# Position products of the two convolutional attentions: queries also kept with image row and column exchanged, every copy made by GpSimd

## The reference, cut to what matters

```
r_q = q.reshape(b, NH, h, w, hd)
rel_h = jnp.einsum('bnhwc,hkc->bnhwk', r_q, Rh)
rel_w = jnp.einsum('bnhwc,wkc->bnhwk', r_q, Rw)
bias = (rel_h[..., :, None] + rel_w[..., None, :]).reshape(b, NH, hw, hw)
attn = jnp.einsum('bnqd,bnkd->bnqk', q, k) * scale + bias
```

## Time and profile before

| | |
|---|---|
| Median of three runs | 3370.66 us |
| The profiled execution's own time | 3370.78 us |
| Its span | 3368.9 us |
| Busy | TensorE matmul 2764.8, VectorE 2414.6, ScalarE 1860.7, GpSimd 435.2 us |
| Mean granted TensorE clock | 0.882 |
| c0: first position product, last one, first load of the next stage | 97.3, 183.1, 195.63 us |
| c1: the same | 1288.2, 1374.3, 1386.79 us |

### The profile page before, as it was taken

How to read it: one execution, slowest core, us unless ns; L and a number is a source line. 1 busy time by engine, 2 the same in 40 slices (tenths; PEclk the granted TensorE clock), 3 DMA queues, 4 the chain that set the end, 5 groups by cost and what they waited for, 6 DMA issues and landing times. The chain is left out here.

```text
span 3368.9 us, 62705 instructions
## 1 busy us (share of the span) xinstructions
PE 2764.8 (82%) x18708; PEld 1277.7 (38%) x18708; DVE 2414.6 (72%) x4597; ACT 1860.7 (55%) x2592; POOL 435.2 (13%) x513
## 2 busy tenths in 40 slices
PE   5948999997499239589999956199999959599999
PEld 3612222226499126222222234022222236366666
DVE  6458999974766354579999955589999835465665
ACT  4416777773255124167777736067777736465554
POOL 0010111111333510101111110201111100000000
PEclk9759999996699667599999977599999979699999
DMA  2555776664122214567766701101111110200000
GB/s 64 169 125 114 151 148 142 148 126 143 33 78 76 70 31 146 134 110 150 149 146 149 145 22 50 57 28 52 48 48 49 48 32 1 55 22 5 9 5 14
DMA packets 202070, 277.27 MB, mean 82 GB/s; under 512 B 54302, under 2 KB 93454, under 8 KB 201930
## 3 DMA queue, kind: packets, MB, share of 16 engines
q1 hardware_dynamic: 162346, 211.32, 27.1%
q0 software_dynamic: 19920, 31.57, 4.0%
q10 hardware_dynamic: 19664, 32.60, 3.3%
HBM read 196.93 MB, written 77.46 MB: 81 GB/s over the span
## 5 line engine op out<-in xcount | busy, mean ns | idle before, releaser
L750 DVE TENSOR_REDUCE c1att_mx<-c1att_m 128x1 f32<-128x512 f32 x768 | 493.4, 685 | 35.7 <-PE c1att_m L688 30.6
L750 DVE TENSOR_REDUCE c0att_mx<-c0att_m 128x1 f32<-128x512 f32 x768 | 493.4, 685 | 32.5 <-PE c0att_m L688 27.2
L750 DVE TENSOR_REDUCE f1att_mx<-f1att_m 128x1 f32<-128x512 f32 x768 | 493.3, 685 | 26.5 <-PE f1att_m L688 21.8
L996 ACT ACTIVATE c1att_p<-c1att_s 128x1024 f32<-128x1024 f32 x384 | 373.9, 1020 | 152.0 <-PE c1att_s L703 151.9
L996 ACT ACTIVATE c0att_p<-c0att_s 128x1024 f32<-128x1024 f32 x384 | 373.9, 1020 | 148.8 <-PE c0att_s L703 148.7
L996 ACT ACTIVATE f1att_p<-f1att_s 128x1024 f32<-128x1024 f32 x384 | 373.9, 1020 | 143.8 <-PE f1att_s L703 142.8
L1426 ACT ACTIVATE moe_h<-moe_u,moe_bu 128x512 f32<-128x512 f32 x192 | 136.5, 711 | 175.6 <-PE moe_u L1343 93.9
L688 PE MATMUL f1att_m<-f1att_km,f1att_qm 16*128 16x512 f16 x768 | 155.7, 401 | 88.6 <-DVE f1att_ka L959 52.9
L716 PE MATMUL f1att_o<-f1att_p,f1att_vs 128*32 128x512 f32 x1536 | 206.2, 609 | 0.6 <-ACT f1att_p L996 0.6
L716 PE MATMUL c0att_o<-c0att_p,c0att_vs 128*32 128x512 f32 x1536 | 206.2, 609 | 0.6 <-ACT c0att_p L996 0.6
L716 PE MATMUL c1att_o<-c1att_p,c1att_vs 128*32 128x512 f32 x1536 | 206.1, 609 | 0.6 <-ACT c1att_p L996 0.6
(11 more groups left out here) (608 smaller groups left out, 5430.8 us busy)
## 6 DMA issues: line engine op xcount, KB each, us to landing
xt<-rel_parts SPq DMA_DIRECT2D x256, 128.0 KB, 5.0
xt<-qk_parts SPq DMA_DIRECT2D x192, 128.0 KB, 4.4
y<-rel_parts SPq DMA_DIRECT2D x128, 128.0 KB, 5.6
y<-qk_parts SPq DMA_DIRECT2D x96, 128.0 KB, 5.1
c0att_qm<-rel_parts SPq DMA_DIRECT2D x144, 64.0 KB, 2.1
c1att_qm<-rel_parts SPq DMA_DIRECT2D x144, 64.0 KB, 2.1
expert_rows<-y SPq DMA_DIRECT2D x39, 192.0 KB, 2.0
o_sums<-c0att_o ACTq DMA_DIRECT2D x24, 256.0 KB, 4.3
```

What stands on the lines that cost most here:

```text
L750: dve.tensor_reduce(mx[:, n:n + 1], bank[:, :], AX.X, ALU.max).then_inc(s_mx, 1)
L996: act.activation(pr[h][kt % 2][:, :], sps[h][:, :], ACT.Exp).then_inc(s_e, 1)
```

## The change

The stage keeps a second set of the queries, `by_x`, in which each quarter is stored column by column. It lies in `parts`, whose chunk c is free once the chunk's matmuls are done. Rows 0 to 63 of `by_x[g]` take the high part, rows 64 to 127 the low part (which comes from rows 0 to 63 of `low`). GpSimd makes all 48 copies of 64 x 512 elements. The table `th[1]` holds its values in both halves of its rows, by one more ScalarE activation, so one matmul gives high table by (high + low) query. For k = 1 two matmuls take the place of three, and they read runs of 16 neighbouring elements. TensorE waits, at the beginning of each (g, 1), for the copies of that group's last chunk.

```
+        s_byx = [m.sem(f"byx{k}") for k in range(2)]
+        by_x = parts
+        def by_columns(t, c):
+            return t[:, c * CHUNK:(c + 1) * CHUNK].rearrange("p (s x y) -> p s x y", s=2, x=QSIDE)
+        def by_rows(t, c, g):
+            return t[0:GW, at(c, g)].rearrange("p (s y x) -> p s x y", s=2, y=QSIDE)
@@ GpSimd
-                for i, t in enumerate(th + tl if rel else ()):
+                if not rel:
+                    return
+                for i, t in enumerate((th[0], tl[0], tl[1])):
                     pool.memset(t[GW:P, :], 0.0).then_inc(s_zero, 1)
                     pool.wait_ge(s_zero, i + 2)
+                for c in range(CHUNKS):
+                    pool.wait_ge(s_v, 4 * c + 4)
+                    for g in range(GROUPS):
+                        pool.wait_ge(s_hi, c * GROUPS + g + 1)
+                        pool.tensor_copy(by_columns(by_x[g][0:GW, :], c), by_rows(high, c, g)).then_inc(s_byx[0], 1)
+                        pool.wait_ge(s_lo, c * GROUPS + g + 1)
+                        pool.tensor_copy(by_columns(by_x[g][GW:P, :], c), by_rows(low, c, g)).then_inc(s_byx[1], 1)
@@ TensorE
-                pe.wait_ge(s_zero, 5)
+                pe.wait_ge(s_zero, 4)
+                pe.wait_ge(s_wh, 5)
...
                     for k in range(2):
+                        if k:
+                            for part in s_byx:
+                                pe.wait_ge(part, (CHUNKS - 1) * GROUPS + g + 1)
...
-                                pe.matmul(out, wh, row_of(top, k, r), start=True, stop=False)
-                                pe.matmul(out, wl, row_of(top, k, r), start=False, stop=False)
-                                ins = pe.matmul(out, wh, row_of(rest, k, r), start=False, stop=True)
+                                if k:
+                                    both = column_of(by_x[g], r)
+                                    pe.matmul(out, wh, both, start=True, stop=False)
+                                    ins = pe.matmul(out, wl, both, start=False, stop=True)
+                                    continue
+                                pe.matmul(out, wh, row_of(top, r), start=True, stop=False)
+                                pe.matmul(out, wl, row_of(top, r), start=False, stop=False)
+                                ins = pe.matmul(out, wh, row_of(rest, r), start=False, stop=True)
@@ ScalarE
+                        act.activation(th[1][GW:P, :], tab[1][:, :], ACT.Identity).then_inc(s_wh, 1)
@@
+def column_of(q, r):
+    return q.rearrange("p (n s x y) -> p s x n y", s=2, x=QSIDE, y=QSIDE)[:, r // QSIDE, r % QSIDE]
```

More of the change, by code:

```diff
@@ L492, in _, with row_of @@
                     store_rel(act, GROUPS - 1, 1, qq // 2, qq % 2, 0, rhi)
[L495 to L499, removed]
+def row_of(q, r):
+    return q.rearrange("p (b u s y x) -> p u y b s x", b=B, u=2, s=2, y=QSIDE)[:, r // QSIDE, r % QSIDE]
+def column_of(q, r):
+    return q.rearrange("p (n s x y) -> p s x n y", s=2, x=QSIDE, y=QSIDE)[:, r // QSIDE, r % QSIDE]
 def row_bank(bank, k, j):
```

## The result

The changed kernel takes 3337.62 us (median of 4 runs, 3336.11 to 3344.65), the one before 3371.62 us (4 runs) beside it: ratio 0.9902, 95% interval 0.9886 to 0.9918. The forecast was 3332 us with a range of 3316 to 3360. The span fell from 3368.9 to 3334.5 us, by 34.4.

The account below looks back on a forecast made before the run. TensorE's k = 1 matmuls, reading elements 32 bytes apart, were taken to bound the position products. Saving 19.6 us in each of c0 and c1, 39.2 in all, took 3370.8 to 3332 us, range 3316 to 3360.

Parts of the forecast that it names:

- The copy: GpSimd's 48 copies a stage: 1.10 us each, 0.92 for stepped reads at 1.80 ns an element plus 0.18 fixed.
- the lower bound: GpSimd's copy without any penalty for the 32-byte step: 512 x 0.83 ns + 180 ns = 0.61 us.
- B: Rival: GpSimd copies of 1.5 us; gain only 6.5 us a stage, 3358 us; chance 0.15.
- C: Rival: GpSimd copies of 1.97 us; slower, 3399 us; break-even where the 44th copy ends at 149 us; chance 0.11.
- D: Rival: the step costs GpSimd nothing, copies of 0.61 us; gain 27 us a stage, 3317 us; chance 0.13.
- The lock: Chunk phase: GpSimd copies and VectorE's two-SBUF-input `low` exclude each other for whole instructions, 1.10 + 0.69 = 1.79 us a unit.
- rival A: GpSimd takes two turns to VectorE's one in the chunk phase; gain 11.2 us a stage, 3348 us; chance 0.14.
- The chunk phase: VectorE's 24 units cost 0.16 us more each, 3.8 us in all; the phase ends at 101 us instead of 97.
- All 96 stores lie behind 126 us: End of the stage: 48 stores from each queue take 44.8 us at 281 GB/s, ending at 171.3 us.
- The wait at g = 2: ScalarE's wait for the stores of (0, 0) is over by then, as SP issues them from 126 to 134 us.
- Runs of 16: TensorE's k = 1 matmuls: 0.06 to 0.11 us instead of 0.23, so 67 us of a stage shrink to about 16.
- Rival E: k = 1 matmuls get only fewer, not faster; gain 4.3 us a stage, 3362 us; chance 0.05 with other no-change ways.

Follow-up runs that it names:

- e1: Changed kernel with copies in row order, so k = 1 matmuls read with the 32-byte step again: 3344.61 us, ratio 0.9909 to the kernel before.
- e9: Changed kernel with GpSimd's copies begun only after all 24 remainders (`low`) of the chunk phase: 3380.49 us, ratio 1.0013 to the kernel before.
- e3: Changed kernel with VectorE making the 24 low-part copies, GpSimd only the high-part ones: 3349.13 us, ratio 0.9917 to the kernel before.
- e2: Changed kernel with a third k = 1 matmul, by a table of zeros, back in each row: 3338.88 us, ratio 0.9887 to the kernel before.
- e5: Changed kernel with the query and key scratch laid out so a store's target is one run of 64 rows: 3293.14 us, ratio 0.9767.
- e6: Kernel before the change with only the query and key store layout of one 64-row run: 3344.13 us, ratio 0.9921 to the kernel before.
- e4: Changed kernel in the order (0,0), (1,0), (0,1), (1,1), (2,0), (2,1): 3335.52 us, ratio 0.9887 to the kernel before.
- the first four experiments: e1, e2, e3 and e9, each an edit of the changed kernel, run on one chip: ratios 0.9909, 0.9887, 0.9917 and 1.0013.

## Why the prediction was right, and where it was off

| step, c0 | predicted | measured |
|---|---|---|
| a copy alone | 1.10 us | 1.09 to 1.11 |
| copy and `low` together | 1.79 us | 1.52 |
| first product | 101 us | 102.1 |
| (0, 1) begins | 125 | 121.08 |
| SP's 48 remainder stores | 44.3 us | 44.4 |
| next stage | 176 | 176.60 |
| gain in c0, c1 | 19.6, 19.6 us | 19.0, 12.3 |

**The copy.** The choice between 0.61 and 1.97 us, on which four of the six cases hung, was right. e1 shows the lower bound to be the exact price without the step, 0.61, so the step costs about 0.48 us in 512 elements: (1.09 - 0.18) / 512 = 1.78 ns each against 0.84. By the 2.9 cycles an element of the Trainium skill, GPSIMD Engine Reference, section Performance pitfalls for Q7 kernels, it would have been 1.42 us, an estimate; the measurement decides against that for a plain copy. Its surcharge of one cycle for the step agrees (0.94 ns, 1.1 of the 1.2 GHz cycles of that estimate). Rivals B, C and D fall with it. e9 moved the start of (0, 1) late by another way, and the change broke even about where C said.

The time of c0 is a weaker test of this price than it looks. SP's remainders go out behind its first 48 stores, and these end at 128.4 us with the change, at 131.4, 128.8 and 128.3 in e1, e3 and e9, however long the copies take. In e3 (0, 1) begins at 125.7 instead of 121.1 us and the stage takes 119.8 us instead of 118.2. So any price that brings the 44th copy in before about 126 us should have given nearly this time; it is the copies' own durations that bear the price out.

**The lock.** The collision is there, as e9 shows, and it spares the values (L450), which take 0.34 us as before. A copy and a `low` on their own make 1.10 + 0.69 = 1.79 us, the pair takes 1.52: the two instructions overlap for 0.27 us and do not exclude each other for their whole length. That is against my reading of the earlier trace rows. The Trainium skill, SBUF — State Buffer, section Who interferes with whom, calls it an exclusive lock; taken for the whole of both instructions, the trace does not bear that out. Of the 0.27 us up to 0.18 could be the copy's fixed part, so whether the two still take turns while they move elements stays open. Nor did GpSimd take two turns to one (rival A): copies and `low` alternate one to one. The 44th copy was done at 121.0 us, 4 us sooner than forecast.

**The chunk phase.** 3.8 us were forecast for an even slowing, and the last `low` came 4.1 us later. The sum was right, its parts not. Three pairs make 4.56 us, which is less than the 4.89 us that a chunk took before, so the steady phase isn't slower. The delay arises in the first chunks: 2.2 us at chunk 1's first `low`, 3.7 at chunk 2's, 5.0 at chunk 3's, of which 1.0 comes back. The first part can be read on VectorE's timeline and ScalarE's:

```profile
61.61 1.09 DVE L459 TENSOR_TENSOR c0qkv_low<-c0qkv_qt,c0qkv_high 128x512 f16<-128x512 f32 x1 [0.54 <-ACT c0qkv_high L496]
...
62.90 2.29 DVE L466 TENSOR_TENSOR c0qkv_tab<-c0qkv_raw,c0qkv_own 64x252 f32<-64x252 f32 x2
...
67.88 1.15 DVE L459 TENSOR_TENSOR c0qkv_low<-c0qkv_qt,c0qkv_high 128x512 f16<-128x512 f32 x1 [2.42 <-ACT c0qkv_high L496]
...
72.25 1.39 DVE L472 TENSOR_TENSOR c0qkv_tl<-c0qkv_tab,c0qkv_th 64x252 f16<-64x252 f32 x2
```

```profile
65.22 0.72 ACT L501 ACTIVATE c0qkv_th<-c0qkv_tab 64x252 f16<-64x252 f32 x2 [3.64 <-DVE c0qkv_tab L466]
65.96 0.41 ACT L502 ACTIVATE c0qkv_th<-c0qkv_tab 64x252 f16<-64x252 f32 x1
```

The same instructions of VectorE in the kernel before:

```profile
62.79 0.73 DVE L438 TENSOR_TENSOR c0qkv_tab<-c0qkv_raw,c0qkv_own 64x252 f32<-64x252 f32 x2
...
69.18 0.73 DVE L444 TENSOR_TENSOR c0qkv_tl<-c0qkv_tab,c0qkv_th 64x252 f16<-64x252 f32 x2
```

VectorE's two products for the tables (L466, L438 before) also have two inputs in SBUF. They took 0.73 us before and take 2.29 beside the first copies. ScalarE waits 3.64 us for them where it waited 1.68, and the new activation adds 0.41. I had written that the copies collide with the `low` and with nothing else in this stage; this was the other thing, and I had left it at nothing. Of chunk 2's further 1.5 us the tables' remainders (L472, L444 before) make 0.66. Chunk 3's further 1.3 us come from the pairs: chunk 2 had taken 3.52 us from `low` to `low` before, less than three pairs, and takes 4.81 now. These are readings of the two timelines; no run takes one of them away.

**The end.** "All 96 stores lie behind 126 us" was the step that gave the result, and it holds but for ScalarE's first four. ScalarE's share began at 122 and SP's at 128.4, and SP's 48 took the forecast time, at 1.09, 0.89 and 0.79 us each rather than at an even 0.92. e2 shows that a third matmul doesn't count in it, e5 that the stores do, and e6 that they did not before the change. The wait at g = 2 was not over, as I had said; ScalarE stood for 1.87 us:

```profile
145.63 0.60 ACT L516 ACTIVATE c0qkv_rhi<-c0qkv_rp 128x512 f16<-128x512 f32 x1 [1.87 <-DMA rel_parts<-c0qkv_rlo]
```

It lies beside transfers at a share of 0.92, while SP's queue runs on without a gap, so it can have cost little.

**Runs of 16.** The premise that they make the k = 1 matmuls cheap is right: 0.055 us at the high clock and 0.11 at the low one, against 0.23. The inference that the gain comes from it was not tested in the prediction, and e1 refutes it for this kernel: with the step left in and one matmul of three gone the time is the same. Rival E had priced that at 4.3 us a stage, since it let (0, 1) begin at 125 us; copies without the step let it begin at 103.4. The exchange makes matmuls cheap and copies dear in equal measure at this bound.

**The missing 4.8 us.** The forecast named a gain of 39.2 us, the spans show 34.4. c0 gave 19.0, c1 12.3; the stages between lost 1.7, and from there to f1's first `low` it took 4.5 less (674.0 us before, 669.5 after; in the ten experiments 669.7 to 672.8, so it varies by itself). These 4.5 us are luck: no step of the prediction has them. The term that was off is c1's, 12.3 us where 19.6 were forecast. Its 48 stores of queries and keys took 1.37 us each. The change alone isn't the reason: e2 does the same copies and stores, and its c1 took 120.8 us with 1.28 a store; e1 and e3 took 118.8 and 121.3. In e4 it was 1.47 a store and 126.4 us. About 2 of the 6.4 us come from the two further stores beside ScalarE's. Why the stores before that took 1.26 us in this stage and 1.17 in c0 stays open.

## What to carry to other kernels

Before a bound engine is relieved, work out when its new inputs are ready and what drains behind it: here a 4-fold cheaper matmul was worth 19 and 12 us in its two stages and not 50, since the copies and SP's first stores set the start and the other stores the end, and a smaller edit (one matmul fewer, the step kept) reached the same time. A reordering that gains next to nothing while the stores bind is worth 6 us in c0 when they are spread over more DMA engines, so an edit is tried again after each change of the bound. And when two engines are to work on SBUF side by side, look for all their instructions with two SBUF inputs, the rare ones too.

## What the hardware showed that I had not expected

- GpSimd and VectorE, both reading SBUF, slow each other but overlap: copy 1.09 to 1.46 us, `low` 0.69 to 1.32, one of each in 1.52. Two small instructions of 64 x 252 went from 0.73 to 2.29 us in one place and to 1.39 in another.
- A 32-byte step costs GpSimd a factor of 1.8 (0.61 to 1.09 us for 64 x 512 float16) and TensorE 4.2 (0.055 to 0.231 us for 128 columns), both ending near 1.8 ns an element.
- The shape in which a store's target is written decided its time: 1.24 us for 4 x 16 rows, 0.60 us for 64 rows, with the same 128 KB.
- The same stores took 1.20 to 1.47 us each in different stages and executions of these kernels, and the change's last few in each stage, beside ScalarE's stores, 2.2 to 2.3 us. For the rest of the spread I could find no cause in the trace.
- Outside the changed stage, the time from c0's next stage to c1's first `low` was 1062.7 to 1065.3 us in the profiles of the first four experiments and 1053 to 1061 in all others, which is why kernels are compared here by their ratio to the kernel before on the same chip.
